# Key lists by folded maxima and minima, host-packed weights, x projected in row halves, and a reordered schedule in a one-core conv plus graph-attention kernel

## The reference, cut to what matters

```python
# x (1,128,32,64); a gated pair layer is added to x (_L0_conv_ref), then:
def _forward(x, edge_index, W_gat, att_src, att_dst, b_gat, ...):   # 4096 tokens, but M = 16*1024 in the
    h = (x_flat @ W_gat).reshape(M, HEADS, NUM_EXPERTS)             # full form; ids past the last clamp
    src = concatenate([edge_index[0], loops]); dst = concatenate([edge_index[1], loops])
    e = leaky_relu(a_src[src] + a_dst[dst], 0.2)
    ee = exp(e - segment_max(e, dst)[dst]); denom = segment_sum(ee, dst)
    agg = segment_sum(h[src] * (ee / denom[dst])[:, :, None], dst) + b_gat
    scores = layernorm(agg, gamma, beta).reshape(M, HEADS, EXPERTS).mean(1)
    w = softmax(top_k(scores, 2)); out = sum over 4 experts of gate * (gelu(x @ W1 + b1) @ W2 + b2)
```

## Time and profile before

| | us |
|---|---|
| median of 3 runs | 688.8 |
| lowest, highest | 686.55, 695.03 |
| span of the profiled execution | 685.3 |
| busy in it: VectorE | 441.8 |
| TensorE matmul | 285.6 |
| GpSimd | 282.7 |
| ScalarE | 158.4 |
| mean granted TensorE clock | 0.628 of full |

### The profile page before, as it was taken

The page is one execution under the profiler, slowest core; times in us unless marked ns, Lnnn a source line. Parts: engine busy times, 40 slices in busy tenths (PEclk is TensorE's granted clock), DMA queues, the critical chain, the costliest instruction groups (busy, mean ns, idle before and its releaser), DMA issues. The chain is left out here.

```text
span 685.3 us, 4407 instructions
## 1 busy us (share of the span) xinstructions
PE 285.6 (42%) x1195; PEld 167.5 (24%) x1195; DVE 441.8 (64%) x1112; ACT 158.4 (23%) x304; POOL 282.7 (41%) x289
## 2 busy tenths in 40 slices
PE   0027794796738602220211111124064767599000
PEld 0012363583424200000000000001043544376000
DVE  6997889778799985111261121179999980550897
ACT  0725542222023416332201211229000000000100
POOL 9767592001000677777776776000000077200053
PEclk9999978697655955555555555556555555555555
DMA  9910000000000000100101111000001111000001
GB/s 232 217 31 0 0 1 18 26 1 1 0 0 25 8 10 10 10 10 10 11 10 10 10 10 10 0 0 0 0 1 80 46 11 10 4 1 0 1 0 61
DMA packets 28701, 15.20 MB, mean 22 GB/s; under 512 B 24020, under 2 KB 27172, under 8 KB 28164
## 3 DMA queue, kind: packets, MB, share of 16 engines
q1 hardware_dynamic: 20836, 11.96, 7.0%
q0 software_dynamic: 6608, 2.82, 4.7%
q10 hardware_dynamic: 1232, 0.13, 0.2%
HBM read 10.93 MB, written 3.96 MB: 22 GB/s over the span
## 5 line engine op out<-in xcount | busy, mean ns | idle before, releaser
L545 POOL DMA_INDIRECT stage_c<-node_rows,senti x160 | 151.1, 945 | 116.7 <-DVE senti L1339 66.6
L961 PE MATMUL bank<-stage_a 128*128 128x128 bf16 x384 | 99.1, 435 | 55.8 <-DVE stage_a L1418 44.3
L961 PEld LDWEIGHTS bank<-stage_a 128*128 128x128 bf16 x384 | 67.7, 178 | 87.0 <-DVE stage_a L1418 45.5
L936 PE MATMUL bank<-xnT,w1s 64*128 64x512 f32 x64 | 28.5, 982 | 138.5 <-issue 100.9
L561 POOL DMA_INDIRECT stage_c<-slot_rows,taili x32 | 30.2, 944 | 130.5 <-DMA slot_rows<-stage_c 121.0
L1418 DVE TENSOR_TENSOR stage_a<-bank,bdc 128x8192 bf16<-128x8192 bf16 x12 | 52.5, 4422 | 28.4 <-remote 27.0
L737 ACT ACTIVATE stage_a<-stage_a,rows 128x176 f32<-128x176 bf16 x128 | 46.1, 434 | 53.7 <-DVE stage_a L1363 23.4
L1083 DVE MATCH_REPLACE8 stage_c<-stats,stage_c 128x128 f32<-128x128 f32 x80 | 21.9, 279 | 52.1 <-issue 52.1
L1073 DVE MAX8 stats<-stage_c 128x8 f32<-128x128 f32 x96 | 23.1, 289 | 44.5 <-issue 22.2
L936 PEld LDWEIGHTS bank<-xnT,w1s 64*128 64x128 f32 x64 | 7.1, 269 | 144.8 <-issue 103.0
L1302 DVE MAX8 stage_c<-bank 128x8 f32<-128x176 f32 x128 | 34.9, 332 | 8.3 <-PE bank L896 7.9
(11 more groups left out here) (331 smaller groups left out, 689.5 us busy)
## 6 DMA issues: line engine op xcount, KB each, us to landing
stage_a<-in_L_conv_protein_pair SPq DMA_DIRECT2D x8, 512.0 KB, 7.6
stage_c<-node_rows,senti POOLq DMA_INDIRECT x160
stage_c<-in_L_ffn_edge_index SPq DMA_DIRECT2D x2, 1024.0 KB, 6.9
slot_rows<-stage_c SPq DMA_DIRECT2D x1, 1344.0 KB, 4.6
xin<-in_x SPq DMA_DIRECT2D x1, 1024.0 KB, 12.8
out<-xin SPq DMA_DIRECT2D x2, 352.0 KB, 2.7
stage_c<-slot_rows,taili POOLq DMA_INDIRECT x32
slot_rows<-stage_c SPq DMA_DIRECT2D x1, 480.0 KB, 2.5
```

The costliest lines, as they stand in the source:

```text
L545: g.indirect_dma_start(out=gath[:, l, :], out_offset=None, in_=node_rows[:, :], in_offset=bass.IndirectOffsetOnAxis(ap=locali[:, 2, l:l + ...
L936: mm = p_.matmul(bank[q][:, :], w1s[E * q:E * (q + 1), e, :], xnT[E * q:E * (q + 1), 4 * b:4 * b + 4, :].rearrange("p t n -> p (t n)"), st ...
L961: mm = p_.matmul(pair_ps, high[:, :, c], low[:, :, c], start=(b == 0 and c == 0), stop=(b == OHB - 1 and c == PAIRS - 1))
```

## The change

- `compact` goes away. The 2048 keys are folded in four levels: the larger of two halves goes on, the smaller becomes a list (1024, 512, 256, 128 wide) of which 16, 24, 32 and 48 are taken. With the last level's 128 larger ones they make an unsorted list of 248. The first `merge` goes; the exchange shows 248 keys instead of 176.
- The clamped keys go through a similar network (`clamped_rest`) after the index: 640 places instead of 768, so five blocks.
- The host lays the weights out: `early_w` in one DMA on SyncE's queue, `late_w` in one on GpSimd's. VectorE only scales them.
- x is projected by row halves (K = 64), the compound pairs in one bank of 128 rows instead of four of 32; ScalarE makes their diagonals in 16 copies.
- Order: GpSimd's clamped products behind the divides of x; features among the group sums; eight pair banks behind the second normalisation and ahead of the exchange; after the exchange the places are split (0 and 1 kept, 2 and 3 to 40, the rest to 8), then merged; `dslot` sums after the clamped list; scan of part 0 ahead of the fifth one-hots, scans 1 and 2 behind the flag.

```diff
-CH1, TAKE1 = 128, 24
+FOLDS = (1024, 512, 256, 128)
+TAKES = (16, 24, 32, 48)
+LIST = FOLDS[-1] + sum(TAKES)
+TAKE23, TAKE4 = 40, 8
+W2 = 2 * P + TAKE23 + TAKE4
-CH3, TAKE3 = 128, 48
+W3 = 640
-SCAN_BEFORE = (1, 2, 2)
+SCAN_BEFORE = 4
-    BANK_EVERY, BLOCK_EVERY = 2, 2
+    BANK_EVERY, BLOCK_EVERY = 2, 1
...
+        sp.dma_start(early_w[:, :], early).then_inc(params_in, 16)
...
+        g.dma_start(late_w[:, :], late).then_inc(late_in, 16)
...
             for n in which:
                 center(n)
+            for n in which:
+                divide(n)
             if which[0] == 0:
                 clamped_keys()
-            for n in which:
-                divide(n)
...
+        def compound_diagonals():
+            act.wait_ge(bank_read, NX + 1)
+            act.wait_ge(diagonals_zero, 1)
+            for r in range(4):
+                for c4 in range(4):
+                    ins = a_.activation(bdc[C * c4:C * (c4 + 1), :, c4, r:NC:4],
+                                        cpw[C * r:C * (r + 1), :, c4:C:4].rearrange("k t g -> k g t"), ACT.Copy)
+            ins.then_inc(bdc_ready, 1)
...
+            for h in range(2):
+                for q in range(2):
+                    half = slice(E * q, E * (q + 1))
+                    mm = p_.matmul(project_bank(n + q)[:, 3 * E * h:3 * E * (h + 1)], tT[half, b, m + h, :],
+                                   bdz[half, q, :], start=False, stop=True, skip_group_check=True)
...
-        compact(work, cand1[:, :], CH1, NCH1, TAKE1, first=lambda: dve.wait_ge(keys_counted, 1))
+        for n, width in enumerate(FOLDS):
+            source = work if n == 0 else larger_of[n - 1]
+            larger = larger_of[n] if width > FOLDS[-1] else cand1[:, 0:width]
+            a, b = source[:, 0:width], source[:, width:2 * width]
+            v.tensor_tensor(larger, a, b, ALU.max).then_inc(vec, t.up())
+            v.tensor_tensor(smaller_of[n], a, b, ALU.min).then_inc(*((keys_folded, 1) if n == 0 else (vec, t.up())))
+            settle()
+        def sweep_keys(r, replace):
+            taken = FOLDS[-1]
+            for n, (take, width) in enumerate(zip(TAKES, FOLDS)):
+                if r < take // 8:
+                    top = cand1[:, taken + 8 * r:taken + 8 * r + 8]
+                    if not replace:
+                        v.max(top, smaller_of[n]).then_inc(vec, t.up())
+                    elif r < take // 8 - 1:
+                        v.match_replace(smaller_of[n], top, smaller_of[n], 0.0).then_inc(vec, t.up())
+                taken += take
+            settle()
...
+        v.tensor_scalar(scaled, scaled, affine[:, 0:1], None, ALU.mult).then_inc(weights_scaled, 1)
+        v.tensor_scalar(bdlas, bdlas, affine[:, 2:3], None, ALU.mult).then_inc(weights_scaled, 1)
...
+            if n == 5:
+                sweep_keys(3, False)
...
+            elif n == 6:
+                make_features()
...
+        for n in range(NX, EARLY):
+            read_bank(n)
...
-                v.max(coll[:, 8 * k:8 * k + 8], bank[4 + m % 2][:, SLOTS * r:SLOTS * (r + 1)]) \
+                v.max(coll[:, 8 * k:8 * k + 8], bank[4 + m % 2][:, LIST * r:LIST * (r + 1)]) \
...
+        token_scale()
...
+        for r in range(TAKE23 // 8):
+            v.max(cand2[:, 2 * P + 8 * r:2 * P + 8 * r + 8], third).then_inc(vec, t.up())
...
-        compact(clamped, ccand, CH3, NCH3, TAKE3, between=between_sweeps, rounds=range(1, TAKE3 // 8))
+        clamped_rest()
...
+        for h in range(HEADS):
+            dve.wait_ge(weighted, h + 1)
+            v.tensor_reduce(dslot[:, h], segd[:, h % 2].rearrange("p j l -> p l j"), AX.X, ALU.add).then_inc(dslot_done, 1)
...
         for b in range(OHB):
-            for n, at in enumerate(SCAN_BEFORE):
-                if at == b:
-                    scan_part(n)
+            if b == SCAN_BEFORE:
+                scan_part(0)
             onehots(b)
...
         dve.wait_ge(last_in, 16)
+        for n in range(1, len(PARTS) - 1):
+            scan_part(n)
         own_scores(t)
```

More of the change, by code:

```diff
@@ L160, in build @@
     dst_ok = ktmp
+    f1_ = carve(stage_b[:, EC:3 * EC])
+    larger_of = [f1_(n) if n > FOLDS[-1] else None for n in FOLDS]
+    smaller_of = [f1_(n) for n in FOLDS]
     b1_ = carve(stage_b)
@@ L253, in build @@
     ccand = stats[:, 0:W3]
+    left = clamped
+    hp1, hq1 = work[:, 0:1024], work[:, 1024:2048]
+    hp2, hq2, hr, fs = (left[:, 512 * n:512 * (n + 1)] for n in range(4))
+    hx, fy = work[:, 0:512], work[:, 512:1024]
+    hq3, hx1, fx2 = (work[:, 1024 + 256 * n:1280 + 256 * n] for n in range(3))
+    hm, hn = left[:, 0:256], left[:, 256:512]
+    hb, hz, fw, fc = (left[:, 512 + 128 * n:640 + 128 * n] for n in range(4))
+    CLAMPED_TAKES = ((fc, 40), (fw, 16), (fx2, 24), (fy, 32), (fs, 8))
     cidx = work[:, W3:2 * W3].bitcast(I32)
@@ L843, in _ @@
         pe.wait_ge(copied, 5)
-        for k in range(NCP):
-            project_comp(NX + k, 0, k)
+        project_comp(NX, 0)
         turn_tiles(6)
@@ L1175, in merge @@
                 settle()
-        read_after = (5, 6, 7, 8, 10, 11, 13, 14, 16, 17, 19, 20)
-        merge(cand1, sent, lambda r: read_bank(NX + read_after.index(r)) if r in read_after else None)
-        outer, middle, inner, top_i = (keyi[:, n] for n in range(1, 5))
-        mid_i, bottom_i = senti[:, 0], senti[:, 1]
-        outer_at, middle_at, inner_at, far = local[:, :], tgt[:, :], head[:, :], reset[:, :]
-        v.tensor_scalar(keyi[:, 0], sent[:, :], -1.0, None, ALU.add).then_inc(vec, t.up())
```

443 lines of the change are left out of this document (216 added, 227 removed).

## The result

The new kernel takes 688.7 us, median of 19 runs (678.05 to 690.07); the kernel before, run beside it, 691.6 (686.55 to 700.09, 19 runs). The ratio is 0.989, 95% interval 0.985 to 0.993: 1.1% faster, less than half of the 2.6% that I forecast. The medians differ by 0.4% only: the runs of the new kernel lie in clusters, near 678, 685 and 689 us, whose cause stayed open, and every ratio in this text leaves out the runs more than 1.5% above the fastest of their kernel, here the uppermost cluster, to which the profiled execution belongs. The profiled execution spans 686.9 us, against 685.3.

What follows compares the result with a forecast made beforehand. Gathers were taken to hold back every engine's issue by 1.4 us each. First gather 224, one-hots 236 later, histogram 92.6, tail 68 and output 47.1 gave a span of 667.7 us, so a median of 671.2; range 646 to 700.

Steps and rivals of the forecast that it cites:

- What bounds the kernel: Whole kernel: each gather holds back issue for all engines by 1.4 us, from some 37 us after the first.
- the crawl's end: End of the slow stretch beside the 160 gathers, where all engines issue slowly: 224 us after the first gather.
- The front: Start to the exchange: second normalisation at 92 to 93 us, exchange starting at 117.5 instead of 125.7.
- the exchange: The 64-step key exchange: 80.5 us instead of 70.5, as each of its 128 MAX8 grows to 248 elements.
- The port lock: Front: VectorE instructions with two SBUF inputs wait for GpSimd's SBUF reads; bias chain ends near 52 us, without it near 43.
- the bias chain's end: Front: nine little VectorE steps, each able to wait for GpSimd, end at 52 us, as before; bounds 43 and 54.
- The banks: Pair banks between second normalisation and exchange: 25 us, bounds 20 and 29; before, 31.5 us.
- Through the gathers: First gather to first one-hots: 236 us instead of 268.2, the expert loop one unit ahead and ending about with the crawl.
- The slower rival (d): Expert loop: exposed tail without a lead, first one-hots 268 us after the first gather, 703 us in all; chance 0.12.
- Histogram: After the first one-hots: five blocks instead of six, 92.6 us instead of 138.5, TensorE clock staying at 0.50.
- tail: Histogram's end to final chain: scans 1 and 2, store and 32 tail gathers now exposed, 68 us instead of 5.9.
- Rival (c): Gathers: no crawl in the new kernel, the histogram runs beside them, 541 us; chance 0.04.

Runs made afterwards that it cites:

- scans_early: New kernel with the scan of part 0 ahead of the second pair of one-hots, parts 1 and 2 ahead of the third: 662.7 us.
- products_first: New kernel with GpSimd's two multiplications of the clamped keys ahead of the divides, as in the kernel before: 687.6 us, 0.989 of the kernel before.
- Half_turns: New kernel with two of the four transposes that turn each expert output back left out: 678.1 us.
- weigh_last: New kernel with all 128 weighings behind the expert loop instead of 12 in each unit: 720.3 us.
- gathers_after_9: New kernel with the first gather held until nine of sixteen expert units passed ScalarE, weighings 19 to a unit from the tenth: 647.2 us.
- combined: New kernel with the edits of gathers_after_9 and products_first, and one scan ahead of each of the third, fourth and fifth pair of one-hots: 605.5 us.
- spaced_135: New kernel with a GpSimd memset of 128 elements behind each of the 160 gathers, meant to issue one every 1.35 us: 634.8 us.

## Why the prediction was right or wrong

- **What bounds the kernel** was read rightly: "I take each gather as 1.4 us of held-back issue for all engines". The 1.40 us and the crawl's end (224.2 us after the first gather, 224 forecast) held. "From some 37 us after the first" holds for VectorE alone (34.6 us in the new kernel). ScalarE and TensorE starve from about 7 us on (gaps of 1.85, 3.67 and 5.73 us from 227.9). In the kernel before ScalarE was waiting for the segment mask then and so showed nothing.
- **The front** was within 3 us at each step but the exchange. The port lock put the bias chain's end at 51.7 (forecast 52); the Trainium skill's rule (SBUF — State Buffer, Who interferes with whom) for two-input instructions is now shown on folds too: 2.38 us for 512 elements beside the centring and 0.68 alone, 4.60 for 256 beside a product and 0.42 alone. The banks took 27.65 us where I had 25. The exchange was 5.1 us shorter than forecast, though its 128 MAX8 grew as priced (407 ns from 332, 9.6 us); VectorE was idle for 11.1 us of it instead of 14.2. Some 2.8 of the 5.1 are luck: scans_early has the same program up to there, and from its first MAX8 (122.05) to the last group of them (195.14) it took 73.1 us at a granted clock of 0.73, the new kernel (120.55 to 190.88) 70.3 at 0.82. The rest was not followed up. (A slip without weight: the sweeps have 26 MAX8 and MATCH_REPLACE8, not 31.)
- **Through the gathers** is the step that failed, 261.9 us for 236: "The earlier mask puts it one unit ahead when the crawl begins, and then it ends about with the crawl". Both halves are wrong.
  The mask did not set the end in either kernel; TensorE's place did. In the kernel before TensorE's instructions were handed over while ScalarE stood at the mask, so the three steps of a unit then ran in one go, and ScalarE caught up at its own 16 slots a unit (270.54 to 292.94, 22.4 us = 16 x 1.40). TensorE in the kernel before, then in the new one:

```profile
281.79 2.08 PE L936 MATMUL bank<-xnT,w1s 64*128 64x512 f32 x4 [16.91 <-remote]
283.80 1.98 PE L945 MATMUL bank<-owner_w,w2s 128*64 128x512 f32 x4
285.70 1.12 PE L954 MATMUL bank<-ident,tT 128*128 128x128 f32 x4
```

```profile
262.68 2.08 PE L922 MATMUL bank<-xnT,late_w 64*128 64x512 f32 x4 [11.45 <-issue]
272.61 1.97 PE L931 MATMUL bank<-hid,late_w 128*64 128x512 f32 x4 [7.84 <-ACT tT L709]
283.71 1.11 PE L940 MATMUL bank<-ident,tT 128*128 128x128 f32 x4 [9.13 <-issue]
```

  The new kernel's first GELU is 7.6 us ahead of its first gather (213.68, 221.24), the old one's was 10.2 ahead (215.42, 225.57): the gathers came forward 2.6 us further than the loop did, which is one unit of 2.66, and the loop lost that unit. This loss is in part chance: in scans_early and products_first, the same program up to there but for the order of the products, the lead was 9.9 us, no unit was lost, and the one-hots came 256.2 and 256.3 us after the first gather.
  And "ends about with the crawl" leaves out the units behind it. The old kernel had three left at the crawl's end, so one unit ahead would have left two. With two fewer than the four of the new kernel, at 6.2 us each, the term is 249.6 and not 236: 13.6 us of the miss are this, 12.3 the unit not won and the one lost. Half_turns, weigh_last and gathers_after_9 show that the count of instructions and TensorE's place set the loop's end.
- **The slower rival (d)** had the mechanism: "the loop's own issue sets its pace, and a silent VectorE gives it nothing". Its price, 268, was 6 us too high: in the kernel before the last destination sum began at 484.26, 8.7 us after the last weighing, because VectorE had a sweep and the index to do between. I gave it 0.12, because the earlier trace rows end in destination sums on VectorE. The 31 us a unit that I read were a mean of units of 22.4 and of 33.6 us; the later ones (353.17 to 386.77, 24 x 1.40) would have told.
- **Histogram** (92.2 for 92.6, clock 0.50) and **tail** (64.7 for 68) were right, in mechanism and size. That the tail speaks against the change is confirmed: 34 us by the place of the scans.
- **Rival (c)**, no crawl, was put at 541 us and is what 0.2 us more between two gathers bring: 566. The trace of before held the hint, an issue every 1.25 us against a crawl of 1.40 a gather, and I read both numbers without asking what the difference meant.

## What to carry to other kernels

When everything beside a row of indirect gathers moves in equal steps, count instructions in them, of the engine with the most: that sets the end, not the busy time. Then look at the spacing of the gathers before moving work around them; here 0.2 us more between two of them took 122 us off the median, seven times what I forecast for the whole change. And when a change brings forward the start of such a stretch, ask what ran cheaply just before it.

## What the runs showed of the hardware

- Indirect gathers issued every 1.25 us hold each other engine to one instruction per 1.40 us (a matmul and its weight load are two; in the histogram they came somewhat faster), until 160 x 1.40 us after the first one. TensorE in the expert loop starved from some 7 us after the first, ScalarE in gathers_after_9 from 20 us, VectorE from 35 us. At 1.45 us or more between them (1.35 is between the two) the other engines run at full pace. Neither the count of rows nor a limit of four outstanding changes it.
- Instructions that an engine has already been handed run at full pace in the crawl: 37 to 39 matmuls (9.6 to 10.0 us) in three runs (gathers_after_9, combined, spaced_135). Behind the first tail gather the histogram ran on for 22.5 us in combined and 29 in the kernel before.
- A small VectorE instruction beside a GpSimd product of 2048 elements can last as long as the product: 3 x 256 elements, 0.41 us alone, 4.60 us beside it.
